# A linear-attention layer and a mixture of experts on one core: mix products left in PSUM until the input is added, shared expert on the routed experts' buffers, first weights loaded apart, stores issued by SyncE, and a new order of the pipelined stage

## The chip, the core and the metric

The kernel runs on one core of a Trainium2 chip. Its engines are TensorE (PE in the rows; PEld is its weight load), VectorE (DVE), ScalarE (ACT), GpSimd (POOL) and SyncE (SP), which here only issues transfers. Each engine runs its own instructions in program order and waits on semaphores for the others. Time is device time in microseconds (us); less is better. All data is fp32.

## What is computed

The input is 32 sequences of 256 tokens with 128 channels. Cut to what matters:

```
delta = shift(h) - h                          # the token before, minus this one
x1    = tanh(tanh((h + delta*mu) @ xl_w1.T) @ xl_w2.T + b)       # 5 groups of 32
mus   = einsum(x1, x_out_w) + x_bias          # five mixes r, w, k, v, g
r, k, v, g = (h + delta*mus_i) @ {r,k,v,g}_w.T
w     = tanh((h + delta*w_mu) @ w_w1.T) @ w_w2.T + w_b;  wd = exp(-exp(w))
scan over t:  o = r.S + sum(r*bonus*k)*v;   S = S*wd + k v
attn  = (groupnorm(o) * gn_w + gn_b) * silu(g) @ o_w.T
x     = layernorm(h + attn)
out   = layernorm(x + shared_ffn(x) + sum over the top 2 of 16 experts of weight * ffn_e(x))
```

Each expert is 128 to 512 to 128 channels with a ReLU.

## The kernel before

**Three stages.** In the first (to about 543 us) the tokens go through attention, router and shared expert in 16 units of two sequences (512 tokens); each token's row is scattered to DRAM at the place of its expert. In the second (to 856 us) 80 tiles of 256 rows go through their experts. In the third the two results of each token are read back, added and normalized, 16 units again.

**The first stage is a software pipeline.** A unit's work is cut into steps (a_: mixing and projections; b_: the scan, as five levels of products that double their length; c_: group norm, layer norm, router, slots, scatter; f_: shared expert). Each engine has a `body` that lists its steps with an offset. `pipeline(body)` runs the body once per i, and `at(d, step)` calls the step for unit i + d. I call one run of the body in the steady state a frame: one step of each kind, for several units. So the order of the work is written out by hand in the bodies; nothing reorders it later. `done(eng, name, u)` waits until unit u has raised that semaphore; `before(eng, name, u)` waits for the unit before it (or further back).

**The steps that matter here.** `a_adapt0` (PE, from the input tile hT), `a_adapt1`, then five products `mix` into the PSUM banks P0 and P1. VectorE's `a_mul` computes (product + bias) * delta and `a_add` adds the input; the sum `mixed` feeds the projections `a_r`, `a_decay_hid`, `a_k`, `a_v`, `a_g`. GpSimd's `b_step` 0 to 4 build the scan's levels, each waited for by PE's `b_level`, and each but the first waits for the level before. `c_attn` (PE) gives the attention output, and `c_z` (VectorE) adds the residual h_res. SyncE's loop issues for each u: the load of hT for unit u, a piece of expert weights, the load of h_res for unit u-1, which waits for `z` of unit u-2, and a padding row write; then it comes to hT of unit u+1. So the load of hT for unit X+3 stands behind `z` of unit X in SyncE's queue.

**Buffers.** The shared expert's hidden layer `hid` and the zero-filled v_flat and norm_work lie in the tile that later holds the experts' first weights (w_sb in the rows), so those weights are loaded in four pieces, each when its part is free. In the rows `w_ring` holds R, the scan's receptance.

Of the kernel before, what the change touches and what calls it, by code (L numbers as in the profile page):

```python
# [55 lines left out]
EARLY_COLS = MAT_AT["o_w"]  # L56


def build(nc, hidden, hidden_t, mats_dram, cols_dram, masks_dram, w1_dram, w2_dram, b2_dram, out):
# [8 lines left out]
    with ctx:  # L68
# [92 lines left out]
        hid = w1_flat[:, 2 * VD + 4 * UT:2 * VD + (4 + HC) * UT].rearrange("p (c t) -> p c t", t=UT)  # L161
# [18 lines left out]
        row_in = [rows[i // 4][i // 2 % 2][:, i % 2 * SUB:(i % 2 + 1) * SUB, :] for i in range(RING)]  # L180
        xTe = [x1T[0][:, i * ST:(i + 1) * ST] for i in range(2)]
        hide = two("hide", [128, HC, ST])
# [32 lines left out]
        def pipeline(body):  # L215
            for i in range(-2, UNITS + 3):
# [11 lines left out]
        def _(sp):  # L228
            sp.dma_start(mats[:, 0:EARLY_COLS], mats_dram[:, 0:EARLY_COLS]).then_inc(sem("weights"), 16)
            sp.dma_start(cols[:, :], cols_dram).then_inc(sem("weights"), 16)  # L230
# [10 lines left out]
            sp.wait_ge(sem("hT_edge"), 1)  # L241
            load_h(0)
# [3 lines left out]
            load_h(1)  # L246
            sp.wait_ge(sem("pad_rows"), 1)
# [4 lines left out]
            sp.dma_start(b2_sb[:, :, :], b2_dram).then_inc(sem("b2_in"), 16)  # L252
# [12 lines left out]
            at = lambda n: n // (HIDDEN + HC)  # L265
            done(sp, "o_ps", UNITS - 2)
# [13 lines left out]
            def load_rows(j, i):  # L280
                if not (isinstance(j, int) and j < RING):
                    sp.wait_ge(sem(f"e_back{i // 2}"), (j - i) * (2 * SUB * 16 // RING))
                for t in range(2):
                    sp.nop(nofuse=True)
                    r = sp.value_load(tile_ri[0:1, bass.ds(j + t, 1)], min_val=0, max_val=EXPERTS * CAP)
                    sp.dma_start(row_in[i + t], rows_dram[bass.ds(r, ST), :].rearrange("(s p) c -> p s c", p=128)).then_inc(sem(f"e_rows_in{i // 2}"), 16)
            for j in range(0, RING, 2):
                load_rows(j, j)
# [10 lines left out]


        @block.tensor
        def _(pe):
            mm = nc.tensor.matmul
            pe.wait_ge(sem("weights"), 32)
# [19 lines left out]
            def a_adapt0(u):  # L324
                if u == 0:
                    pe.wait_ge(sem("xl_parts"), 2)
                before(pe, "gate", u)
# [19 lines left out]
            def a_mix_w_r(u):  # L347
                done(pe, "adapt1a", u)
# [32 lines left out]
            def a_mix_g(u):  # L381
                done(pe, f"mul{MIX_V}", u)
# [152 lines left out]

            def body(at):
                at(1, a_mix_w_r)
                at(-1, c_attn)
                at(-2, f_up, 3)
                at(1, a_decay_hid)  # L540
                at(0, b_level, 3)
                at(1, a_w)
                at(1, a_r)
                at(-2, f_down, 0)
                at(0, b_level, 4)
                at(1, a_mix_k_v)
                at(-2, f_down, 1)
                at(1, a_mix_g)
                at(0, b_k_tok)
                at(-1, c_turn)  # L550
                at(1, a_k)
                at(0, b_kv)
                at(-1, c_logits)
                at(0, b_o_near)
                at(1, a_g)
                at(0, b_o_far)
                at(1, a_v)
                at(-1, f_up, 0)
                at(2, a_adapt0)
                at(1, b_level, 1)  # L560
                at(1, b_level, 0)
                at(-1, f_up, 1)
                at(2, a_adapt1)
                at(-1, c_place)
                at(-1, f_up, 2)
                at(1, b_level, 2)
# [66 lines left out]
        def _(act):  # L633
            A = nc.scalar.activation
            act.wait_ge(sem("weights"), 32)
# [158 lines left out]
            def body(at):  # L794
                at(-1, a_w)
                at(-1, a_r)
                at(-3, c_x1)
                at(-2, b_k_tok)
                at(-3, c_x1T)
                at(-1, a_k)  # L800
                at(-2, b_chunk_decay)
                at(-1, a_k_near)
                at(-1, a_decay)
                at(-1, a_r_near)
                at(-1, a_g)
                at(-3, c_logits)
                at(-2, b_o)
                at(-2, c_sq)
                at(-1, a_v)
                at(-3, f_hid, 0)  # L810
                at(0, a_adapt0)
                at(-3, f_hid, 1)
                at(-3, c_rows1)
                at(0, a_adapt1a)
                at(0, a_adapt1b)
                at(-2, c_aff)
                at(-3, c_top_exp)
                at(-3, f_hid, 2)
                at(-3, f_hid, 3)
                at(0, a_decay_hid)  # L820
# [41 lines left out]
            def f_store(u):  # L862
                done(act, "f_out", u)
                act.dma_start(out_v[:, u * TILES:(u + 1) * TILES, :], f_out[u % F_RING]).then_inc(sem(f"stored{u % F_RING}"), 16)  # L864
            for u in range(UNITS):
                f_norm(u)
                f_store(u)
            for i in range(F_RING):
                act.wait_ge(sem(f"stored{i}"), UNITS // F_RING * 16)
# [3 lines left out]
        def _(pool):  # L873
# [16 lines left out]
            pool.wait_ge(sem("weights"), 32)  # L890
# [514 lines left out]
```

## Time and profile before

| | us |
|---|---|
| median of 3 runs (lowest, highest) | 910.92 (910.13, 914.22) |
| the profiled execution's own time | 908.88 |
| its span, first to last instruction | 906.8 |
| mean granted TensorE clock | 0.946 of full |
| busy: PE, DVE, ACT, POOL | 785.1, 512.3, 491.9, 564.6 |

Busy shares are means over three stages of different kind. A PE that is busy is not always at its peak; the time in which it has nothing is what counts. "idle before" in a row is the engine's idle time ahead of the instruction, and the name behind the arrow is what ended it. SPq and ACTq are the queues by which SyncE and ScalarE issue transfers.

### The profile page before, as it was taken

The numbers are of one execution on the slowest core, as the hardware profiler recorded it, in microseconds if no ns is written. First come the engines' busy times: TensorE is split into PE (matmuls) and PEld (weight loads), VectorE is DVE, ScalarE is ACT, GpSimd is POOL, SyncE is SP. The second block draws the span as 40 slices with busy tenths as digits, with TensorE's granted clock in tenths as the row PEclk, the third lists the DMA queues.
The fourth block names the chain that finished last, engine by engine and source line by source line (L and its number), as shares of the span: only waits on it lengthen the run. The fifth ranks groups of instructions, "written<-read, shape, count | busy, mean of one in ns | idle before, by whom it ended". The sixth has DMA issues, their size and how long they took to land. (4 is left out here: it accounts for less than half of the span.)

```text
span 906.8 us, 24200 instructions
## 1 busy us (share of the span) xinstructions
PE 785.1 (87%) x8068; PEld 568.7 (63%) x8069; DVE 512.3 (56%) x1496; ACT 491.9 (54%) x1153; POOL 564.6 (62%) x709
## 2 busy tenths in 40 slices
PE   4687989988998899888987858999999999999493
PEld 1243545644565555554655537999999999999441
DVE  2436887889788978788775432333333333333076
ACT  1344667556655566555654314666555666566346
POOL 3334788788778787888788471555555554555444
PEclk9967999999999999999998678999999999999887
DMA  4001102211122112210213323222222222221294
GB/s 161 24 2 42 42 26 60 66 55 34 46 67 57 35 48 61 64 51 26 61 43 98 113 67 94 71 70 65 73 69 71 62 65 66 67 68 47 66 357 135
DMA packets 70244, 63.43 MB, mean 70 GB/s; under 512 B 8051, under 2 KB 61561, under 8 KB 70033
## 3 DMA queue, kind: packets, MB, share of 16 engines
q1 hardware_dynamic: 52496, 41.06, 15.9%
q0 software_dynamic: 9216, 17.07, 5.7%
q10 hardware_dynamic: 8448, 4.20, 1.6%
q8 instruction: 52, 0.85, 0.4%
q14 instruction: 32, 0.25, 0.1%
HBM read 38.75 MB, written 25.63 MB: 71 GB/s over the span
## 5 line engine op out<-in xcount | busy, mean ns | idle before, releaser
L974 POOL DMA_INDIRECT expert_results<-yw_all,rows x160 | 155.5, 972 | 155.3 <-ACT yw_all L837 130.6
L829 ACT ACTIVATE hide<-psB,w_ring 128x256 f32<-128x256 f32 x320 | 125.6, 475 | 67.9 <-PE psB L588 67.9
L599 PEld LDWEIGHTS psO<-w_sb,hide 128*128 128x128 f32 x1280 | 155.3, 192 | 4.6 <-issue 0.6
L599 PE MATMUL psO<-w_sb,hide 128*128 x1280 | 156.0, 275 | 0.1
L943 POOL DMA_INDIRECT dispatched_rows<-rows,slot x128 | 130.2, 1017 | 38.0 <-issue 31.0
L588 PE MATMUL psB<-x1T,w_ring 128*128 128x256 f32 x640 | 152.8, 382 | 0.2 <-DVE x1T L1264 0.2
L1277 DVE TENSOR_TENSOR K<-psO,b_sb 128x256 f32<-128x256 f32 x80 | 34.0, 425 | 175.1 <-PE psO L599 175.1
L588 PEld LDWEIGHTS psB<-x1T,w_ring 128*128 128x128 f32 x640 | 116.3, 192 | 13.3 <-issue 0.6
L921 POOL TENSOR_TENSOR w_ring<-w_ring,tot 128x128 f32<-128x128 f32 (+2 forms) x160 | 122.7, 788 | 0.0
L1022 DVE SCALAR_TENSOR_TENSOR mixed<-psP,cols,delta 128x512 f32<-128x512 f32 x80 | 59.7, 747 | 73.3 <-PE psP L318 42.5
L837 ACT ACTIVATE yw_all<-K,rows 128x128 f32<-128x128 f32 x160 | 55.4, 393 | 67.5 <-DVE K L1277 67.5
L792 ACT ACTIVATE w_sb<-psO,cols 128x512 f32<-128x512 f32 x64 | 43.7, 682 | 79.3 <-PE psO L524 78.9
L524 PE MATMUL psO<-x1T,mats 128*128 128x512 f32 x128 | 73.3, 656 | 12.4 <-ACT w_sb L792 12.4
L531 PEld LDWEIGHTS psO<-mats,w_sb 128*128 128x128 f32 x512 | 64.7, 206 | 20.7 <-issue 15.2
L1027 DVE TENSOR_TENSOR mixed<-mixed,hT 128x512 f32<-128x512 f32 x80 | 73.6, 921 | 2.2
L531 PE MATMUL psO<-mats,w_sb 128*128 128x128 f32 x512 | 70.4, 295 | 2.0 <-ACT w_sb L792 2.0
L908 POOL TENSOR_TENSOR tot<-tot 128x128 f32<-128x128 f32 (+4 forms) x80 | 22.2, 278 | 74.7 <-ACT R_near L679 42.3
L928 POOL TENSOR_TENSOR o_rstd<-o_var,minus_half 128x16 f32<-128x16 f32 x16 | 46.9, 2930 | 26.8 <-DVE o_var L1070 26.8
L1271 DVE COPY w_ring<-w_sb 128x516 f32 x80 | 34.4, 429 | 34.0 <-issue 34.0
L309 PE MATMUL psP<-mixed,mats 128*64 128x256 f32 x192 | 35.4, 449 | 19.7 <-DVE mixed L1027 19.7
L426 PEld LDWEIGHTS psB<-w_ring,K 64*32 64x32 f32 x2048 | 20.0, 109 | 47.0 <-issue 45.3
L426 PE MATMUL psB<-w_ring,K 64*32 64x64 f32 x2048 | 30.4, 228 | 17.5 <-POOL w_ring L921 17.5
(173 smaller groups left out, 1320.1 us busy)
## 6 DMA issues: line engine op xcount, KB each, us to landing
rows<-dispatched_rows SPq DMA_DIRECT2D x80, 132.0 KB
w_sb<-expert_results SPq DMA_DIRECT2D x8, 1024.0 KB, 13.0
hT<-in_hidden_t SPq DMA_DIRECT2D x16, 256.0 KB, 4.2
h_res<-in_hidden SPq DMA_DIRECT2D x16, 256.0 KB, 2.9
out<-w_sb ACTq DMA_DIRECT2D x16, 256.0 KB, 2.3
w_sb<-in_w SPq DMA_DIRECT2D x14, 256.0 KB, 4.4
expert_results<-yw_all,rows POOLq DMA_INDIRECT x160, 2.3
dispatched_rows<-pad_rows SPq DMA_DIRECT2D x17, 132.0 KB, 3.5
```

Source lines behind the costliest of these rows:

```text
L426: last = mm(to, k, r, start=True, stop=True, tile_position=(64 * b, 32 * c4))
L524: mm(O1, mat("shared_w1")[:, c * 128:(c + 1) * 128], x1T[u % 2][:, :], start=True, stop=True).then_inc(sem(f"hid_ps{c}"))
L531: last = mm(O1[:, j * 128:(j + 1) * 128], hid[:, c, j * 128:(j + 1) * 128], mat("shared_w2")[:, c * 128:(c + 1) * 128], start=(c == 0), st ...
L588: last = mm(up_ps(p)[:, c // 2, (c % 2) * ST:(c % 2 + 1) * ST], w1b[i % W_RING][:, c * 128:(c + 1) * 128], xTe[p], start=True, stop=True)
L599: last = mm(psO[:, p, s * 128:(s + 1) * 128], hide[p][:, c, s * 128:(s + 1) * 128], w2_sb[:, bass.ds(e, 1), c, :].rearrange("p e c -> p (e ...
L829: last = A(hide[p][:, c, :], psB[:, 2 * p + c // 2, (c % 2) * ST:(c % 2 + 1) * ST], ACT.Relu, bias=w1b[i % W_RING][:, HIDDEN + c:HIDDEN + ...
L837: last = A(yw[i][:, s, :], ye[p][:, s, :], ACT.Copy, scale=row_in[i][:, s, AT_W:AT_W + 1])
L921: last = G.tensor_tensor(r, r, l, ALU.mult)
L943: G.indirect_dma_start(rows_dram[:, :], bass.IndirectOffsetOnAxis(slot[u % 2][:, j, k:k + 1], 0), rows[k][u % 2][:, j, :], None).then_inc( ...
L974: G.indirect_dma_start(back_dram[:, :], bass.IndirectOffsetOnAxis(row_in[i][:, s, AT_DEST:AT_DEST + 1].bitcast(u32), 0), yw[i][:, s, :], N ...
L1022: V.scalar_tensor_tensor(mixed[MIX_BUF[n]][:, :, :], unflat((P0, P1)[MIX_BANK[n]]), col(f"x_bias{n}"), delta[:, :, :], ALU.add, ALU.mult). ...
L1027: V.tensor_tensor(mixed[MIX_BUF[n]][:, :, :], mixed[MIX_BUF[n]][:, :, :], hT[u % 2][:, :, 1:T + 1], ALU.add).then_inc(sem(f"mixed{n}"))
```

## The change

Parts, in the order of the diff below:

- hid lies in the routed experts' `hide` buffers, so the last piece of expert weights (experts 12 to 15) is loaded without waiting for the shared expert; the ring of row buffers is listed in another order, and only its last pair waits for the last `base_out`.
- The first weights (224 of 1160 columns) have a transfer and a semaphore of their own, and the first hT is loaded by ScalarE's queue. VectorE makes xl_prev and xl_cur first.
- `a_mul` writes its result back into the PSUM bank in place, and `a_add` takes it from there; the waits for the `mixed` buffers move from `a_mul` to `a_add`. `a_mix_g` waits for the sum of v instead of its product.
- b2 is added at the start of GpSimd's program and not after its pipeline.
- The stores of the last stage are issued by SyncE, behind its eight loads of expert results, and not by ScalarE.
- All four bodies are written in another order with other offsets.

```diff
-EARLY_COLS = MAT_AT["o_w"]
+FIRST_COLS, EARLY_COLS = MAT_AT["x_out_a"], MAT_AT["o_w"]
...
-        hid = w1_flat[:, 2 * VD + 4 * UT:2 * VD + (4 + HC) * UT].rearrange("p (c t) -> p c t", t=UT)
+        hide_both = sb("hide", [128, 2, HC, ST])
+        hide = [hide_both[:, i, :, :] for i in range(2)]
+        hid = hide_both[:, :, :, :].rearrange("p i c t -> p (i c t)").rearrange("p (c t) -> p c t", t=UT)
...
# sync
-            sp.dma_start(mats[:, 0:EARLY_COLS], mats_dram[:, 0:EARLY_COLS]).then_inc(sem("weights"), 16)
-            sp.dma_start(cols[:, :], cols_dram).then_inc(sem("weights"), 16)
+            sp.dma_start(mats[:, 0:FIRST_COLS], mats_dram[:, 0:FIRST_COLS]).then_inc(sem("first_weights"), 16)
+            sp.dma_start(cols[:, :], cols_dram).then_inc(sem("first_weights"), 16)
+            sp.dma_start(mats[:, FIRST_COLS:EARLY_COLS], mats_dram[:, FIRST_COLS:EARLY_COLS]).then_inc(sem("weights"), 16)
...
+            load_w1(-(-(2 * VD + 4 * UT) // (HIDDEN + HC)), EXPERTS)
...
-            load_w1(at(2 * VD), at(2 * VD + 4 * UT))
-            done(sp, "base_out", UNITS - 1)
-            load_w1(at(2 * VD + 4 * UT), EXPERTS)
+            load_w1(at(2 * VD), -(-(2 * VD + 4 * UT) // (HIDDEN + HC)))
...
+            def f_store(u):
+                done(sp, "f_out", u)
+                sp.dma_start(out_v[:, u * TILES:(u + 1) * TILES, :], f_out[u % F_RING]).then_inc(sem(f"stored{u % F_RING}"), 16)
+            for u in range(UNITS):
+                f_store(u)
...
# tensor: the body (ScalarE's, GpSimd's and VectorE's change in the same way)
-                at(1, a_mix_w_r)
-                at(-1, c_attn)
...
-                at(1, a_v)
-                at(-1, f_up, 0)
-                at(2, a_adapt0)
...
+                at(2, a_k)
+                at(0, c_attn)
+                at(1, b_o_far)
+                at(2, a_g)
+                at(2, a_v)
+                at(2, b_level, 1)
+                at(2, b_level, 0)
+                at(3, a_adapt0)
...
# scalar
+            act.dma_start(hT[0][:, :, 1:T + 1], hidden_t[:, 0:UB, :]).then_inc(sem("h_in0"), 16)
...
# gpsimd: moved from behind pipeline(body) to its front
+            pool.wait_ge(sem("b2_in"), 16)
+            pool.wait_ge(sem("late_weights"), 16)
+            G.tensor_tensor(b2_sb[:, :, :], b2_sb[:, :, :], mat("shared_b2").unsqueeze(1).broadcast_to([128, EXPERTS, C]),
+                            ALU.add).then_inc(sem("b2_ready"))
...
# vector
-                V.scalar_tensor_tensor(mixed[MIX_BUF[n]][:, :, :], unflat((P0, P1)[MIX_BANK[n]]),
-                                       col(f"x_bias{n}"), delta[:, :, :], ALU.add, ALU.mult).then_inc(sem(f"mul{n}"))
+                ps = unflat(psP[MIX_BANK[n]])
+                V.scalar_tensor_tensor(ps, ps, col(f"x_bias{n}"), delta[:, :, :], ALU.add, ALU.mult).then_inc(sem(f"mul{n}"))
...
-                V.tensor_tensor(mixed[MIX_BUF[n]][:, :, :], mixed[MIX_BUF[n]][:, :, :], hT[u % 2][:, :, 1:T + 1], ALU.add).then_inc(sem(f"mixed{n}"))
+                V.tensor_tensor(mixed[MIX_BUF[n]][:, :, :], unflat(psP[MIX_BANK[n]]), hT[u % 2][:, :, 1:T + 1], ALU.add).then_inc(sem(f"mixed{n}"))
```

In a steady frame TensorE comes from `c_attn` of unit X to `a_adapt0` of unit X+3, the pair that SyncE's loop links. Before, `c_attn` (L480) starts the following piece and `a_adapt0` (L332) stands 21 rows behind it:

```order
174 L480 MATMUL psO<-mats,w_sb 128x128 x4
175 L524 MATMUL psO<-x1T,mats 128x512
176 L309 MATMUL psP<-mixed,mats 64x256 x2
177 L426 MATMUL psB<-w_ring,K 32x64 x16
178 L367 MATMUL psP<-decay_hid,mats 64x256 x2
179 L309 MATMUL psP<-mixed,mats 64x256 x2
180 L531 MATMUL psO<-mats,w_sb 128x128 x8
```

The products of the mix, of the scan and of the shared expert follow `c_attn` there. The next piece, also of TensorE before, is the place of `a_adapt0`:

```order
192 L468 MATMUL psB<-state,w_ring 128x32 x14
193 L390 MATMUL psP<-v_wc,mixed 128x128 x4
194 L524 MATMUL psO<-x1T,mats 128x512
195 L332 MATMUL psP<-hT,xl_cur 64x256 x2
196 L332 MATMUL psP<-hT,xl_prev 64x256 x2
197 L426 MATMUL psB<-w_ring,K 32x64 x16
198 L426 MATMUL psB<-R_near,K_near 32x128 x16
199 L524 MATMUL psO<-x1T,mats 128x512
```

It comes ahead of `b_level` 1 and 0 (L426) there.

In the changed kernel the same two steps are `c_attn` (L493) and `a_adapt0` (L343); between them stand `b_o_far` (L481), `a_g` (L409), `a_v` (L403) and two levels (L439):

```order
209 L319 MATMUL psP<-mixed,mats 64x256 x2
210 L493 MATMUL psO<-mats,w_sb 128x128 x4
211 L481 MATMUL psB<-state,w_ring 128x32 x14
212 L409 MATMUL psP<-mixed,mats 128x512
213 L403 MATMUL psP<-v_wc,mixed 128x128 x4
214 L439 MATMUL psB<-w_ring,K 32x64 x16
215 L439 MATMUL psB<-R_near,K_near 32x128 x16
216 L343 MATMUL psP<-hT,xl_cur 64x256 x2
217 L343 MATMUL psP<-hT,xl_prev 64x256 x2
218 L537 MATMUL psO<-x1T,mats 128x512
```

`a_adapt0` has moved from far behind `c_attn` to close behind it, and `b_level` 1 and 0 of the same unit now stand ahead of it.

On VectorE, before, product and sum of the decay mix (L1022, L1027) and of r follow each other, and the sum has two inputs in SBUF:

```order
222 L1022 SCALAR_TENSOR_TENSOR mixed<-psP,cols,delta 128x512
223 L1027 TENSOR_TENSOR mixed<-mixed,hT 128x512
224 L1022 SCALAR_TENSOR_TENSOR mixed<-psP,cols,delta 128x512
225 L1027 TENSOR_TENSOR mixed<-mixed,hT 128x512
226 L1096 TENSOR_TENSOR z<-psO,h_res 128x512
```

In the changed kernel the two products (L1023) come first, r's ahead of the decay's, and both sums (L1034) read PSUM:

```order
242 L1219 TENSOR_SCALAR dest<-dest 128x8
243 L1023 SCALAR_TENSOR_TENSOR psP<-psP,cols,delta 128x512 x2
244 L1034 TENSOR_TENSOR mixed<-psP,hT 128x512 x2
245 L1227 TENSOR_TENSOR base_out<-psO,rows_1 128x512
246 L1059 COPY_PREDICATED pair<-masks,psB 128x32x8
```

The sum of the decay mix is now the fourth of these instructions and no longer the second.

At the end of SyncE's program, before, stand the loads of the results alone (L298):

```order
149 L298 DMA w_sb<-expert_results 128x8x256 x8
150 L68 UNCONDITIONAL_BRANCH
```

Nothing follows them. In the changed kernel the stores do (L304):

```order
148 L291 REGISTER_ALU
149 L291 COMPARE_AND_BRANCH
150 L300 DMA w_sb<-expert_results 128x8x256 x8
151 L304 DMA out<-w_sb 128x4x128 x16
152 L68 UNCONDITIONAL_BRANCH
```

All 16 stores stand behind the eighth load.

## Rows read from the trace of the kernel before

**Rows 1.** Windows, a frame: stretch, us; PE, PEld, DVE, ACT, POOL busy; PEclk, DMA, GB/s

```profile
262.80:292.20 29.40, 26.14 (x372) 15.97 (x371) 24.46 (x67) 17.62 (x38) 23.71 (x32) 1.00 0.18 52
```

**Rows 2.** Lines L1027, L1022 and L1096: ns min/median/max, first and last start

```profile
L1027 DVE TENSOR_TENSOR mixed<-mixed,hT x80: 665/692/2250, 18.2 to 472.7; 128x512 f32<-128x512 f32 x80
...
L1022 DVE SCALAR_TENSOR_TENSOR mixed<-psP,cols,delta x80: 736/750/754, 17.4 to 470.1; 128x512 f32<-128x512 f32 x80
...
L1096 DVE TENSOR_TENSOR z<-psO,h_res x16: 681/682/692, 77.8 to 512.2; 128x512 f32<-128x512 f32 x16
```

**Rows 3.** Timeline, PE, a steady frame: start us, us, engine, line, operation

```profile
265.82 1.12 PE L396 MATMUL psP<-mixed,mats 128*128 128x512 f32 x2
...
269.56 1.02 PE L524 MATMUL psO<-x1T,mats 128*128 128x512 f32 x2
...
271.52 0.46 PE L426 MATMUL psB<-w_ring,K 64*32 64x64 f32 x32
271.85 0.73 PE L426 MATMUL psB<-R_near,K_near 64*32 64x128 f32 x32
...
279.44 1.16 PE L480 MATMUL psO<-mats,w_sb 128*128 128x128 f32 x8
280.44 1.02 PE L524 MATMUL psO<-x1T,mats 128*128 128x512 f32 x2
282.81 0.65 PE L309 MATMUL psP<-mixed,mats 128*64 128x256 f32 x4 [1.35 <-DVE mixed L1027]
```

**Rows 4.** Timeline, VectorE and SyncE's queue, the same frame

```profile
283.97 0.68 DVE L1096 TENSOR_TENSOR z<-psO,h_res 128x512 f32<-128x512 f32 x1
...
285.97 0.37 SPq L235 DMA_DIRECT2D hT<-in_hidden_t  x1
```

**Rows 5.** Transfers of hT: one issue of that frame; then all 16, us to landing

```profile
hT<-in_hidden_t SPq DMA_DIRECT2D x1, 256.0 KB, 4.5
...
DMA to landing us min/median/max: 2.6/4.2/6.8
```

**Rows 6.** Timeline, ScalarE: table load for unit 0, first tanh of units 2 and 15

```profile
9.70 1.28 ACT L642 ACT_TABLE_LOAD   x1 [9.70 <-PE psP L332]
...
67.28 0.38 ACT L642 ACTIVATE adapt<-psP 128x256 f32<-128x256 f32 x1
...
449.77 0.38 ACT L642 ACTIVATE adapt<-psP 128x256 f32<-128x256 f32 x1
```

**Rows 7.** Timeline, GpSimd, the end of its first stage

```profile
489.94 1.21 POOL L921 TENSOR_TENSOR w_ring<-w_ring,tot 128x256 f32<-128x256 f32 x2
...
538.10 0.96 POOL L943 DMA_INDIRECT dispatched_rows<-rows,slot  x1 [0.30 <-issue]
```

**Rows 8.** Timeline, GpSimd, the last memset of the start

```profile
5.33 1.83 POOL L889 MEMSET w_sb<- 128x2048 f32 x1
```

**Rows 9.** Timeline, between the first and the second stage

```profile
541.04 0.37 SPq L264 DMA_DIRECT2D w_sb<-in_w  x1
...
548.12 1.08 PE L579 MATMUL psP<-mats,rows 128*128 128x128 f32 x4 [7.94 <-DMA rows<-dispatched_rows]
```

**Rows 10.** Timeline, SyncE's queue, ScalarE and VectorE in the last stage

```profile
855.62 18.45 SPq L298 DMA_DIRECT2D w_sb<-expert_results  x8
...
878.36 1.65 ACT L858 ACTIVATE w_sb<-w_sb,f_shift,f_rstd 128x128 f32<-128x128 f32 x4 [0.54 <-DMA out<-w_sb]
...
879.76 0.69 DVE L1305 TENSOR_TENSOR w_sb<-psO,base_out 128x512 f32<-128x512 f32 x1
...
881.84 0.69 DVE L1305 TENSOR_TENSOR w_sb<-psP,base_out 128x512 f32<-128x512 f32 x1
```

**Rows 11.** Windows of the last stage

```profile
862.00:864.00 2.00, 2.00 (x4) 0.77 (x3) 0.00 (x0) 0.00 (x0) 0.00 (x0) 0.50 1.10 353
```

**Rows 12.** DMA issues, the last stage's loads and stores: KB each, median us to landing

```profile
w_sb<-expert_results SPq DMA_DIRECT2D x8, 1024.0 KB, 13.0
...
out<-w_sb ACTq DMA_DIRECT2D x16, 256.0 KB, 2.3
```

More of the change, by code:

```diff
@@ L179, in build @@
         tile_ri = sb("tile_ri", [1, ETILES], i32)
-        row_in = [rows[i // 4][i // 2 % 2][:, i % 2 * SUB:(i % 2 + 1) * SUB, :] for i in range(RING)]
+        row_in = [r[:, i * SUB:(i + 1) * SUB, :] for r in (rows[0][0], rows[1][0], rows[1][1], rows[0][1]) for i in range(2)]
         xTe = [x1T[0][:, i * ST:(i + 1) * ST] for i in range(2)]
-        hide = two("hide", [128, HC, ST])
         ye = [K[i].rearrange("p (s c) -> p s c", c=C) for i in range(2)]
@@ L536, in body @@
             def body(at):
-                at(1, a_mix_w_r)
-                at(-1, c_attn)
[L539 to L556, printed above, removed]
-                at(1, a_v)
-                at(-1, f_up, 0)
-                at(2, a_adapt0)
[L560 to L566, printed above, removed]
+                at(2, a_k)
[6 more added lines that the diff above has]
+                at(3, a_adapt0)
+                at(-1, f_up, 3)
+                at(2, b_level, 2)
+                at(3, a_adapt1)
+                at(-1, f_down, 0)
+                at(3, a_mix_w_r)
+                at(2, b_level, 3)
+                at(-1, f_down, 1)
+                at(0, c_turn)
+                at(3, a_r)
+                at(3, a_decay_hid)
+                at(0, c_logits)
+                at(2, b_level, 4)
+                at(0, f_up, 0)
+                at(3, a_w)
+                at(2, b_o_near)
+                at(3, a_mix_k_v)
+                at(2, b_k_tok)
+                at(0, f_up, 1)
+                at(0, c_place)
+                at(2, b_kv)
+                at(3, a_mix_g)
+                at(0, f_up, 2)
             pipeline(body)
@@ L794, in body @@
             def body(at):
[L795 to L820, printed above, removed]
+                at(1, a_w)
+                at(-2, c_rows1)
+                at(-2, f_hid, 0)
+                at(-1, c_aff)
+                at(0, b_k_tok)
+                at(-2, f_hid, 1)
+                at(-2, c_top_exp)
+                at(0, b_chunk_decay)
+                at(1, a_r_near)
+                at(1, a_k)
+                at(1, a_decay)
+                at(1, a_k_near)
+                at(-2, f_hid, 2)
+                at(0, b_o)
+                at(0, c_sq)
+                at(1, a_g)
+                at(1, a_v)
+                at(2, a_adapt0)
+                at(-2, f_hid, 3)
+                at(2, a_adapt1b)
+                at(2, a_adapt1a)
+                at(-1, c_x1)
+                at(-1, c_x1T)
+                at(2, a_decay_hid)
+                at(-1, c_logits)
+                at(2, a_r)
             pipeline(body)
```

124 lines of the change are left out of this document (60 added, 64 removed).

## The prediction

> **What bounds the kernel now.** I took the chain of waits first. It is a chain in the first stage and the experts' matmuls in the second, where TensorE never pauses. No part of the change alters an instruction of the second stage, so I left it at its time. Then I took the windows of one frame of the first stage. A frame lasts 29.40 us, TensorE is busy for 26.14 of them, GpSimd for 23.71, VectorE for 24.46 [rows 1]. So TensorE idles 3.26 us per frame, and what a new order can win there is nearly that, 16 times. The timeline of the frame shows four such pauses; the longest is 1.35 us, when `a_decay_hid` waits for the sum of the decay mix (L1027) [rows 3].
>
> That sum is the VectorE instruction that varies: its minimum is 665 ns, its median 692, its longest 2250, while the sum of the same shape that takes one input from PSUM (L1096) stays between 681 and 692 in all 16 frames [rows 2]. The long ones fall on GpSimd's `b_step` instructions. The Trainium skill (SBUF — State Buffer, Who interferes with whom) has a rule for it: a VectorE instruction with two SBUF inputs contends with a GpSimd instruction that reads SBUF, and one with at most one SBUF input does not. By that rule every sum of the changed kernel costs about 0.69 us wherever the order puts it; were something else the cause, the long one could stay and bring its pause along, 13 times 1.35 us. L1096 speaks for the rule.
>
> **Part 1, mix products in PSUM.** Five products per frame keep their inputs; only the target changes. The nearest price is the same instruction with an SBUF target, 0.75 us (L1022, 736 to 754 ns [rows 2]). No row has VectorE writing to PSUM: below I bound it by 0.69 (an ordinary sum [rows 2]), above by 0.75 + 0.69 = 1.44, a second pass over the tile. I take 0.75, the row it is nearest to. One of the five sums per frame is a long one (2.25 at most) and comes down to 0.69, which takes 1.5 us per frame off VectorE and removes the cause of TensorE's 1.35 us pause. VectorE isn't the bound, so only the pause counts.
>
> **Part 2, the order.** I laid out one new frame with start-to-start distances of the old one. The chains I checked: mix products (1.13 us) to VectorE's two products and two sums, to `a_decay_hid`, to ScalarE's tanh, copy of r and exponential, to the next mixes; the second pair of mixes to `a_mix_g` and `a_k`; k to `b_step` 0. They fit between TensorE's 26.14 us of work with 0.2 to 0.7 us to spare. GpSimd needs 23.71 plus 0.30 ahead of each of eight scatters [rows 1, 7], 26.1 us; `b_step` 1 now directly follows 0, so it waits for `b_level` 1 in between, about 0.7 us. That makes 26.8 us: the frame's floor if nothing else waited.
>
> What is late next is a transfer. The load of hT for unit X+3 stands behind `z` of unit X in SyncE's queue, and `z` follows `c_attn` of X. Before, `a_adapt0` of X+3 came 20 us after `c_attn` of X, so the load was hidden. Now between their starts lies only this TensorE work: `c_attn` 1.00 (279.44 to 280.44), `b_o_far`, `a_g` and `a_v` 3.74 (three steps, 265.82 to 269.56), `b_level` 1 and 0 1.06 (271.52 to 272.58): 5.80 us [rows 3]. The load's chain is longer: `c_attn` 1.16 to its end [rows 3] and 0.13 to VectorE (a usual hand-over); start of `z` to the issue of hT 2.00 (283.97 to 285.97, with the issues of h_res and the padding ahead) [rows 4]; landing 4.5 in that frame [rows 5]; 0.13 to TensorE. Sum 7.92; in the frame before the second piece was 1.80, giving 7.72. TensorE therefore waits about 2.1 us ahead of `a_adapt0` in every frame: 26.14 - 5.80 + 7.8 = 28.2 us, with 7.8 between the two sums. Behind `a_adapt0` stand f_up 3, `b_level` 2, `a_adapt1` and all that follows; the wait covers the 0.7 us of `b_level` 2's own wait for GpSimd.
>
> The frames that this covers are those from the tanh of unit 2 to that of unit 15: 449.77 - 67.28 = 382.5 us for 13, 29.42 each [rows 6]. At 28.2 they take 366.6: **-15.9 us**. The first two frames are single chains through nearly empty engines; new steps ahead of `a_adapt0` (levels 1 and 0) stand against earlier r: 0, bounds -2 and +2.
>
> **Part 3, start.** The first tanh's table load begins at 9.70 [rows 6], after loads of 580 KB and v's mean. With 112 KB first, xl first and hT on another queue, what holds it next is the `zeroed` wait: the last memset ends at 5.33 + 1.83 = 7.16 [rows 8]. Bounds -2.5 and 0; I take **-2.0**, since nothing else in the trace comes between. b2's addition falls into the time in which GpSimd has no unit yet; uncovered it would cost its own length once, 4.5 us in the timeline.
>
> **Part 4, drain.** GpSimd ends its last `b_step` 3 at 491.15 and its last scatter at 539.06, 47.9 us later [rows 7]. The new order has one more unit's scatters behind that point: four units of eight at 1.26 = 40.3, `b_step` 4 1.6, o_rstd 2.9, two z_rstd 2.6, and about 3 of waiting for the last slots: 50.5 us, +2.6. Against that the way from the tanh of unit 15 to the end of `b_step` 3 shrinks, 41.4 before [rows 6, 7] and about 37 in my layout. Sum **-2.0**, bounds -7 and +4.
>
> **Part 5, to the experts.** The piece of w_sb at 541.04 goes ahead of the rows, and TensorE starts at 548.12, waiting for rows [rows 9]. That 1290 KB transfer (6.1 us to landing) now runs long before. **-1.5**, bounds -3 and 0. The shared expert on the hide buffers costs nothing: no one else uses them then.
>
> **Part 6, last stage.** ScalarE needs 1.65 us for a unit with 0.54 idle before it, 2.18 in all, VectorE starts a unit every 2.08 (879.76, 881.84) [rows 10]. Without ScalarE's issues VectorE sets the pace: 15 times 0.10, -1.5. But SyncE's eight loads of 1 MB end their issue only at 855.62 + 18.45 = 874.07 [rows 10], and they land a median of 13.0 us after issue, the stores on ScalarE's queue 2.3 [rows 12]. The 8.39 MB need, at the 353 GB/s of this stage [rows 11], until about 882. If stores land behind them, unit 4's normalization waits (878.36 before) until about 882.5, and VectorE's unit 8, which needs its buffer, starts at 884.2 and not 881.84 [rows 10]. Less VectorE's faster pace and the ACT lag of 1.7 us, the end moves **+0.5**, bounds -1.5 and +2.5. The Trainium skill (DMA: Bandwidth & Descriptors, Queues, rings and completion order) speaks against this edit: one issuing engine's ring is consumed in order, while an engine takes turns between the rings of two issuers. The 13.0 against 2.3 agrees; without that rule the term would be -1.5.
>
> **Sum.** -15.9 + 0 - 2.0 - 2.0 - 1.5 + 0.5 = -20.9 us against the profiled execution's 908.88 (span 906.8): 888.0. The three runs shown lie 1.3 to 5.3 above that execution, so I say **889 us** for a median.
>
> **Rivals.**
> A: the load isn't waited for. The shortest hT landing is 2.6 [rows 5], 1.9 less, which leaves 0.2; the frame falls to GpSimd's 26.8: another 13 x 1.4 = 18 us, 871. For it: the median of 4.2 includes frames of varied traffic. Against it: 4.5 in the steady frame with the same three neighbours.
> B, slower than before: the same wait, longer. The longest landing is 6.8 [rows 5]; the frame becomes 28.2 + 2.3 = 30.5, +30 us, 919. The point from which it decides is a landing of 6.1 us, where 13 frames of 29.8 eat the other terms. Against it: 6.8 falls in the crowded start.
> C: the slack of the mixes is used up. If a product into PSUM costs 1.44, the four instructions ahead of `a_decay_hid` grow by 1.4 and the second pair likewise, against 0.2 and 0.7 of slack: +1.9, 30.1 per frame, 914. A milder form, 0.8 us of small waits that I have not seen in a frame of some 100 steps, gives 29.0 and 899.
> D: VectorE or GpSimd contend elsewhere as before and the order wins nothing: 13 frames of 29.4, 905.
>
> **How the numbers follow.** Forecast (frame 27.7 to 28.7, 883 to 896): 0.53. A: 0.18. C mild: 0.16. D: 0.05. B and C full: 0.08. Faster by over 0.5% means below 906.4, slower above 915.5; half a percent is about what a measurement of this kernel tells from no change. Faster: 0.53 + 0.18 + 0.16 + 0.02 of D = 0.89; same 0.05; slower 0.06. The range reaches down to A and up to the milder C: 871 to 902; the forecast's own range is 883 to 896.
>
> **What would show it.** First tanh near 9 us. Starts of `a_adapt0`'s tanh 28.2 us apart, TensorE idle about 2 us ahead of it, with the DMA of hT as releaser, and none ahead of `a_decay_hid`. All 80 sums near 0.69, products near 0.75. The last scatter ending near 519, experts unchanged at 3.73 us per tile, ScalarE's fifth unit of the last stage some 4 us late behind a store. Wrong it would be if the frame shows another releaser in TensorE's longest pause, or if the products take over 1 us.

## The result, and the profile after

Over 11 runs of each, the changed kernel takes a median of 902.86 us (896.35 to 910.28) and the kernel before 910.92 (907.75 to 916.80): a ratio of 0.990, 95% interval 0.986 to 0.993. It is faster, but by 8 us and not by the 22 predicted; the median lies just above the range's end of 902. The profiled execution took 897.26 us (span 895.2, mean granted clock 0.942) against 888.0 in the prediction's sum. In a second comparison the ratio was 0.997 (0.993 to 1.000): 910.63 us, 12 runs from 903.56 to 917.09.

The wait that the prediction named is there. In TensorE's waits (us in total, times, longest) it stands first. The matmuls that wait for a sum of the mixes, `a_decay_hid` among them, waited 19.7 us in 14 times before and now 7.1 in 6, all before 99 us:

```profile
PE psP L343 <- DMA hT<-in_hidden_t: 25.5, 13, 2.3
```

The sums and products of the mixes, by line (busy us, mean ns of one), answer to [rows 2]. No sum is over 692 ns, where the longest was 2250, and a product into PSUM costs what one into SBUF did:

```profile
L1023 DVE SCALAR_TENSOR_TENSOR psP<-psP,cols,delta 128x512 f32<-128x512 f32 x80 | 58.5, 749 | 55.9 <-PE psP L328 55.9
L1034 DVE TENSOR_TENSOR mixed<-psP,hT 128x512 f32<-128x512 f32 x80 | 53.5, 685 | 6.9 <-PE psP L319 3.8
```

One frame is now the time from one `a_adapt0` on TensorE to the next. These windows of six frames answer to [rows 1]; the number behind POOL's is the granted clock:

```profile
89.95:120.04 30.09, 25.63 (x337) 13.79 (x337) 19.35 (x57) 16.80 (x37) 15.36 (x24) 0.83 0.11 32
120.04:147.95 27.91, 26.04 (x371) 16.26 (x371) 21.66 (x67) 17.48 (x38) 23.18 (x32) 1.00 0.19 54
147.95:176.21 28.26, 26.03 (x370) 16.26 (x371) 21.68 (x67) 17.48 (x38) 23.57 (x33) 1.00 0.19 54
176.21:206.16 29.95, 27.68 (x371) 16.79 (x371) 21.43 (x67) 17.37 (x38) 23.22 (x32) 0.94 0.18 51
235.72:263.58 27.86, 26.03 (x370) 16.25 (x371) 21.52 (x67) 17.58 (x38) 23.05 (x32) 1.00 0.19 55
263.58:294.96 31.38, 29.14 (x370) 17.98 (x371) 21.53 (x67) 17.49 (x38) 23.96 (x33) 0.89 0.17 49
```

I call the 11 frames from 120.04 to 437.53 settled: the pipeline is full, all have the same instructions, and each starts behind a pause of 1.56 to 2.27 us. Five of them are shown. Six of the 11 have the clock at 1.00 and last 27.85 to 28.26 us, 27.98 on the mean, as predicted (28.2). The other five last 29.11 to 31.38, because TensorE's own busy time grows from 26.03 to 27.6 or 29.1 at a clock of 0.94 or 0.89. I call them fallen and the six clean. Where inside the frame that happens, two-microsecond windows of the last one shown tell:

```profile
265.00:267.00 2.00, 2.00 (x36) 0.61 (x36) 0.29 (x2) 0.76 (x2) 0.73 (x1) 0.51 0.03 8
267.00:269.00 2.00, 2.00 (x9) 0.54 (x9) 1.76 (x8) 0.10 (x1) 1.90 (x6) 0.50 0.00 0
269.00:271.00 2.00, 2.00 (x11) 2.00 (x10) 0.82 (x5) 1.83 (x4) 2.00 (x2) 0.50 0.02 4
271.00:273.00 2.00, 2.00 (x13) 1.49 (x11) 0.00 (x0) 0.96 (x3) 1.24 (x1) 0.79 0.00 0
273.00:275.00 2.00, 2.00 (x47) 1.54 (x44) 1.38 (x3) 0.00 (x0) 0.95 (x3) 1.00 0.00 0
```

From 265.00 on, 1.4 us behind the end of the pause, the clock stands at 0.50, which is 1.2 of 2.4 GHz, and in the window from 273.00 it is back at 1.00. In the frames at 0.94 that stretch is about half as long. The timeline shows, for two other frames, the pause and the same two f_up matmuls (L537) with the clock fallen and with it full:

```profile
294.96 0.65 PE L343 MATMUL psP<-hT,xl_cur 128*64 128x256 f32 x4 [2.23 <-DMA hT<-in_hidden_t]
296.14 2.08 PE L537 MATMUL psO<-x1T,mats 128*128 128x512 f32 x2
...
235.72 0.65 PE L343 MATMUL psP<-hT,xl_cur 128*64 128x256 f32 x4 [2.01 <-DMA hT<-in_hidden_t]
236.74 1.12 PE L537 MATMUL psO<-x1T,mats 128*128 128x512 f32 x2
```

The start, the way to the experts and the last stage (ScalarE's table load, TensorE's first rows, then SyncE's queue, ScalarE's fourth and fifth unit, VectorE's ninth) answer to [rows 6, 9, 10]:

```profile
7.94 1.28 ACT L656 ACT_TABLE_LOAD   x1 [7.94 <-PE psP L343]
...
534.44 0.88 PE L592 MATMUL psP<-mats,rows 128*128 128x128 f32 x4 [5.14 <-DMA rows<-dispatched_rows]
...
841.70 18.52 SPq L300 DMA_DIRECT2D w_sb<-expert_results  x8
860.27 19.96 SPq L304 DMA_DIRECT2D out<-w_sb  x10
...
862.16 1.65 ACT L872 ACTIVATE w_sb<-hide,f_shift,f_rstd 128x128 f32<-128x128 f32 x4 [0.48 <-DVE f_shift L1332]
870.01 5.11 ACT L872 ACTIVATE w_sb<-hide,f_shift,f_rstd 128x128 f32<-128x128 f32 x13 [6.20 <-DMA out<-w_sb]
...
871.75 0.69 DVE L1312 TENSOR_TENSOR hide<-psP,base_out 128x512 f32<-128x512 f32 x1 [3.46 <-issue]
```

Against the kernel before's profiled execution, stretch by stretch:

| term | predicted | measured | from |
|---|---|---|---|
| 13 frames | -15.9 | -6.5 | 376.19 against 382.73, `a_adapt0` of unit 2 to that of 15 |
| first two frames | 0 | -1.5 | 55.54 against 56.99 |
| start | -2.0 | -1.8 | 5.80 against 7.57 |
| drain | -2.0 | -0.8 | last `a_adapt0` to end of last scatter, 90.98 against 91.77 |
| to the experts | -1.5 | -3.1 | 5.93 against 9.06 |
| experts | 0 | -0.2 | 307.26 against 307.50 |
| last stage | +0.5 | +2.3 | 53.5 against 51.2 |
| sum | -20.9 | -11.6 | 897.26 less 908.88 |

The 13 frames are the term that missed. The other six add up to -5.1 where I had -5.0, and that is luck: the way to the experts came out 1.6 us better, the first frames 1.5 better, the last stage 1.8 worse and the drain 1.2 worse.

### The profile page after: what moved, and what is told of

Its sections match the earlier page's. It is cut to its first block, busy times and chain, and to the rows that moved or that the text cites. A ratio compares the mean times of both kernels' runs of the same rounds, so it can differ in the third digit from the quotient of the medians.

```text
span 895.2 us, 24269 instructions
## 1 busy us (share of the span) xinstructions
PE 787.2 (88%) x8068; PEld 572.1 (64%) x8069; DVE 480.6 (54%) x1496; ACT 489.1 (55%) x1153; POOL 558.8 (62%) x709
## 4 chain that ended last, share of the span: by engine, by line
PE 73%; DMA 10%; DVE 5%; issue 4%; POOL 3%; ACT 2%; SPq 2%; DVEq 0%; POOLq 0%; ACTq 0%
PE psO L612 16%; PE psB L601 16%; PE psO L537 7%; DMA hT<-in_hidden_t 7%; PE psP L328 6%; PE psO L544 5%; PE psP L319 3%; PE psB L439 2%; PE psP L592 2%; PE psP L343 2%; PE psB L471 2%; PE psO L493 2%; PE psB L459 2%; POOL dispatched_rows L955 1%; PE psP L352 1%
## 5 line engine op out<-in xcount | busy, mean ns | idle before, releaser
L979 POOL DMA_INDIRECT expert_results<-yw_all,rows x160 | 157.3, 983 | 154.7 <-ACT yw_all L851 130.1
L933 POOL TENSOR_TENSOR w_ring<-w_ring,tot 128x128 f32<-128x128 f32 (+2 forms) x160 | 118.5, 761 | 0.0
L1023 DVE SCALAR_TENSOR_TENSOR psP<-psP,cols,delta 128x512 f32<-128x512 f32 x80 | 58.5, 749 | 55.9 <-PE psP L328 55.9
L537 PE MATMUL psO<-x1T,mats 128*128 128x512 f32 x128 | 78.4, 698 | 2.0 <-ACT hide L806 1.9
L544 PEld LDWEIGHTS psO<-mats,hide 128*128 128x128 f32 x512 | 62.8, 201 | 12.6 <-ACT hide L806 6.0
L544 PE MATMUL psO<-mats,hide 128*128 128x128 f32 x512 | 68.4, 290 | 2.8 <-ACT hide L806 2.8
L806 ACT ACTIVATE hide<-psO,cols 128x512 f32<-128x512 f32 x64 | 43.7, 683 | 34.4 <-PE psO L537 34.2
L1034 DVE TENSOR_TENSOR mixed<-psP,hT 128x512 f32<-128x512 f32 x80 | 53.5, 685 | 6.9 <-PE psP L319 3.8
L328 PE MATMUL psP<-adapt1a,mats 32*128 32x512 f32 x128 | 41.0, 718 | 6.7 <-ACT adapt1a L662 6.0
L439 PEld LDWEIGHTS psB<-w_ring,K 64*32 64x32 f32 x2048 | 20.5, 113 | 40.9 <-issue 39.1
L1059 DVE COPY_PREDICATED pair<-masks,psB 128x256 f32<-128x256 uint32 x64 | 31.9, 498 | 24.9 <-PE psB L439 23.4
```

Source lines behind the costliest of these rows:

```text
L328: mm(ps, w, a, start=True, stop=True, **kw).then_inc(sem(f"mix_ps{n}"))
L537: mm(O1, mat("shared_w1")[:, c * 128:(c + 1) * 128], x1T[u % 2][:, :], start=True, stop=True).then_inc(sem(f"hid_ps{c}"))
L544: last = mm(O1[:, j * 128:(j + 1) * 128], hid[:, c, j * 128:(j + 1) * 128], mat("shared_w2")[:, c * 128:(c + 1) * 128], start=(c == 0), st ...
L933: last = G.tensor_tensor(r, r, l, ALU.mult)
L979: G.indirect_dma_start(back_dram[:, :], bass.IndirectOffsetOnAxis(row_in[i][:, s, AT_DEST:AT_DEST + 1].bitcast(u32), 0), yw[i][:, s, :], N ...
L1023: V.scalar_tensor_tensor(ps, ps, col(f"x_bias{n}"), delta[:, :, :], ALU.add, ALU.mult).then_inc(sem(f"mul{n}"))
```

## The experiments

The theory: the pause of some 2 us in every frame was priced rightly, but behind it TensorE's clock falls in about half of the frames, and that is the miss. The rivals: the frames are long for another reason and the clock falls with it; or it is the late transfer and not the pause. Ratios are to the kernel before, run beside on the same device, with their 95% intervals.

**The changed kernel again.**

> The changed kernel once more, as the measure for the three that run beside it: 0.990 of the kernel before, 897 to 908 us, a mean granted clock of 0.93 to 0.94. The theory (pause and clock): 13 pauses of 1.6 to 2.3 us ahead of a_adapt0, and in some 5 to 7 of the 13 frames a clock that falls behind the pause, so frames of 28 us and of 29.5 to 31.4 us side by side. Were the long frames chance of one execution, this profile would show 13 frames near 28.2.

Measured: 0.997 (0.993 to 1.000), 910.63 us. Of the 11 settled frames five lasted 27.8 to 28.3 at clock 1.00; six were longer, the longest by 6.2 us of TensorE's busy time:

```profile
205.85:240.18 34.33, 32.27 (x370) 20.03 (x371) 21.50 (x67) 17.47 (x38) 22.68 (x32) 0.80 0.15 44
```

The clean frame is a constant of the kernel; how many frames fall, and how far, differs from one execution to the next. The profile of the kernel with its stores by ScalarE (below), whose first stage is the same, has only two fallen frames of 11: its 13 frames take 370.28 us, where the first execution has 376.19 and this one 382.71.

That is a part of the spread of 14 us and not all of it. Of the 16.4 us between the profiled spans of this execution and the first, 6.5 lie in the 13 frames and 7.3 in the drain (98.26 against 90.98). The last of the pauses stands at the drain's start. Here the clock fell behind it, and TensorE's busy time in the drain is 5.2 us longer (77.84 against 72.64); in the first execution it stayed at 1.00 there.

```profile
448.28:452.28 4.00, 4.00 (x18) 2.85 (x17) 2.04 (x11) 2.47 (x6) 4.00 (x6) 0.50 0.00 0
```

**Load hT one unit earlier.**

```
-            for u in range(2, UNITS):
-                load_h(u)
+            load_h(2)
+            for u in range(2, UNITS):
+                if u + 1 < UNITS:
+                    load_h(u + 1)
                 ...
                 load_res(u - 1)
```

> SyncE issues the load of hT one unit earlier, ahead of the load of h_res, so it no longer stands behind the wait for z. Theory (the pause ahead of a_adapt0 and the clock that falls behind it cost 13 x 2.0 and some 9 us): no wait for the load, frames at 26.8 to 27.2 with the clock at 1.00, 13 frames 350 us where the changed kernel has 376: profiled 870 to 876 us, 0.960 to 0.968 of the kernel before. Rival (the load was late, but the frames are held by GpSimd's own chain or the order, the clock falls by itself): the wait goes to another instruction, frames 28 to 29, 890 to 898 us. Rival (only the 2 us go, the clock still falls in half of the frames): frames 27 to 28.5, some 880 us.

Measured: 0.961 (0.958 to 0.963), 876.25 us, all six runs within 3.3 us. The wait for hT is gone, all 11 settled frames last 27.07 to 27.23 at clock 1.00, and the 13 take 352.42:

```profile
222.25:249.32 27.07, 26.34 (x377) 16.12 (x370) 23.25 (x67) 17.63 (x39) 23.48 (x32) 1.00 0.20 58
```

Of the 23.8 us between these 13 frames and the changed kernel's 376.19, the pause itself explains 11 x 0.9 = 9.8, the five fallen frames 149.63 - 5 x 27.98 = 9.7, and the first two of the 13 (58.70 against 54.32) 4.4.

**The pause filled.** Five matmuls stand in front of the wait; the load comes as late as before.

```
                 before(pe, "gate", u)
+                pe.nop(nofuse=True)
+                if u >= 3:
+                    for _ in range(5):
+                        mm(P1[:, 0:256], mats[:, 0:128], mats[:, 0:256], start=True, stop=True)
                 h_in(u)
```

> The changed kernel, with five matmuls of 256 columns into P1 (their result is overwritten by a_adapt0) in front of the wait for hT from unit 3 on, some 1.4 us of work in the place of the pause of 2; the load comes as late as before. Theory (the pause lets the clock fall): clock 1.00 in all 13 frames, each at 27.9 to 28.3, 13 frames some 366 us where the changed kernel has 376; profiled 886 to 889 us, 0.978 to 0.982 of the kernel before, as the prediction had it. Rival (the clock falls for another reason, and the frames are long for it): the same 376 us and 897 us or more, with 0.94 as the mean clock.

Measured: 0.981 (0.979 to 0.984), 895.68 us where the changed kernel beside it took 910.63. The clock stayed at 1.00 in all 11 settled frames. They weren't shorter than the clean frames, because five matmuls cost 2.28 us and not 1.4, and in four frames hT was later still:

```profile
175.62:203.94 28.32, 28.32 (x381) 17.99 (x380) 21.50 (x68) 17.37 (x38) 23.43 (x32) 1.00 0.19 54
232.26:261.69 29.43, 28.40 (x382) 18.02 (x381) 21.38 (x68) 17.60 (x38) 24.29 (x34) 1.00 0.18 52
```

15 us came back from adding work to the engine that is the bound. Of the 15.6 between the two profiled spans 8.9 lie in the 13 frames and 5.7 in the drain.

**The pause filled in part**: two matmuls in place of five.

> The changed kernel with two matmuls in front of the wait for hT in the place of five: by their cost with five (TensorE's busy time 28.32 less 26.04 a frame, 0.46 each) some 0.9 us of work, so a pause of 1.0 to 1.4 us is left of the 2.0, and the load is as late as in the changed kernel. Theory (the length of the pause decides): clock 1.00 in all settled frames, each 27.9 to 28.3, 13 frames 366 to 368 us, 888 to 891 us, 0.974 to 0.978 of before: the predicted time. Rival (the late hT, not the pause, or any filling short of the whole pause fails): falls in about half of the frames as without filling, 0.99 of before.

Measured: 0.974 (0.972 to 0.977), 889.57 us, with pauses of 0.77 to 1.28 us left and the clock at 1.00 in all 11 settled frames; 13 frames take 368.0, where 366.6 was predicted. So with the load as late as in the changed kernel, the predicted frames come once the clock is kept. That the whole meets the predicted 889 is luck besides: the other terms miss by up to 3 us each and add up to -5.1 against -5.0.

```profile
PE psP L347 <- DMA hT<-in_hidden_t: 12.9, 13, 1.3
...
287.65:315.99 28.34, 27.10 (x375) 16.92 (x375) 21.38 (x68) 17.46 (x38) 23.49 (x33) 1.00 0.19 54
```

**A made pause with hT early.** A load of 16 bytes, issued when `b_level` 0 has ended, holds `a_adapt0` back (on top of the early load):

```
+                    done(sp, "level_ps0", u)
+                    sp.dma_start(scratch[:, :], cols_dram[0:1, 0:4]).then_inc(sem("first_weights"), 16)
...
                 h_in(u)
+                if u >= 3:
+                    pe.wait_ge(sem("first_weights"), u * 16)
```

> The early load of hT stays, but from unit 3 on a_adapt0 also waits for a load of 16 bytes that SyncE issues when b_level 0 has ended: hT is there in time, and TensorE pauses 2 to 3 us all the same at the place of the changed kernel's pause. Theory (any pause of this length lets the clock fall in part of the frames, whatever causes it): clean frames of 26.35 + pause = 28.5 to 29.3, and beside them frames 1.5, 3.1 or 6.2 us longer at a clock of 0.94, 0.89 or 0.80; sum of the 13 frames 380 to 390 us, spread of the times 10 us or more, some 0.995 of before. Rival (the clock falls with the late transfer, by what the load of hT does beside TensorE, not with the pause): all frames clean at 28.5 to 29.3, clock 1.00, spread of the times under 4 us.

Measured in the first run: 0.968 (0.963 to 0.973), but on a device on which every frame also had a stop of another kind (below), so it is no answer.

> The pause made by a load of 16 bytes ahead of a_adapt0, hT loaded early, once more; the first run had 13 pauses of 1.40 to 1.55 us at this place beside the stop of 2.5 us at the state, so that it does not tell the two apart. Theory (the clock falls behind a pause, whatever makes it): with this pause alone frames of 26.1 + 1.45 = 27.6, and some of them longer by 1.55 or 3.1 us at a clock of 0.94 or 0.89; since the pause is shorter than the changed kernel's 2.0 fewer may fall: 0 to 5 of 11. Rival (the late hT transfer is what matters): all at 27.6 with clock 1.00.

Measured in the second: 0.967 (0.965 to 0.969), 882.55 us. Pauses of 1.40 to 1.61 us and no fall in 11 frames:

```profile
PE psP L351 <- DMA scratch<-in_cols: 19.0, 13, 1.6
...
229.49:257.02 27.53, 26.03 (x370) 16.24 (x371) 22.02 (x69) 17.67 (x39) 23.32 (x32) 1.00 0.19 56
```

**The same pause, longer**: three such loads in place of one.

> As the kernel with the pause made by a load of 16 bytes (13 pauses of 1.40 to 1.61 us, clock 1.00 in all 11 settled frames, 882.6 us), but SyncE issues three such loads one behind the other and a_adapt0 waits for all three, so the pause grows by two issues of some 0.4 us to 2.2 to 2.4; hT itself is there long before. Theory (a pause of the changed kernel's length makes the clock fall in part of the frames whatever causes it): clean frames of 28.3 to 28.5, some 3 to 7 of 11 longer by 1.55 or 3.1 us at a clock of 0.94 or 0.89, spread of the times over 7 us, 0.98 to 0.99 of before. Rival (the clock falls only where hT comes late): all frames at 28.3 to 28.5 with clock 1.00, spread under 4 us, 13 frames some 370 us, 892 us and 0.977 of before.

Measured: 1.004 (1.001 to 1.006), 916.23 us, 910.64 to 925.41. The pauses are 1.99 to 2.10 us, hT is there long before, and seven of 11 settled frames fall. I had expected a longer pause (2.2 to 2.4) and a smaller loss (0.98 to 0.99). Three frames, clean, fallen and fallen furthest:

```profile
PE psP L352 <- DMA scratch<-in_cols: 26.6, 13, 2.1
...
239.65:267.73 28.08, 26.04 (x370) 16.26 (x371) 21.94 (x68) 17.57 (x38) 23.19 (x32) 1.00 0.20 53
325.43:356.60 31.17, 29.14 (x370) 18.02 (x371) 21.79 (x68) 17.49 (x38) 23.60 (x32) 0.89 0.18 49
356.60:390.92 34.32, 32.28 (x370) 20.04 (x371) 21.88 (x68) 17.47 (x38) 22.93 (x32) 0.80 0.15 44
```

So the late transfer is not the cause; the pause is, whatever makes it. Against the shorter made pause 7.6 us more of waiting (26.6 less 19.0) cost 34 us, each beside a kernel before of 912 to 913. Of the 32.3 between the two profiled spans 26.6 lie in the 13 frames and 6.7 in the drain, whose first quarter has a clock of 0.72 here and of 1.00 there.

**The mixes alone**: the kernel before, with the products in PSUM and a_add of V moved up behind its product.

> The kernel before with the products kept in PSUM and nothing else but a_add of V moved up behind its product. If the prediction's part on the mixes holds by itself: sums at 0.69, no pause ahead of a_decay_hid, 13 frames of 29.42 become 28.1 to 28.4, 0.981 to 0.986 of before. Rival (the 1.35 us turn up in another wait of the old order, since GpSimd's chain or ScalarE ends last there): frames 29.0 to 29.4, 0.995 to 1.0 of before.

Measured first, on the device with the extra stop: 1.009 (1.006 to 1.012).

> The kernel before with the products in PSUM, once more beside the same. The first run gave 1.009 of before with frames of 33.3 and 38.1 side by side, under the stop that the trace calls remote. If the old order has no place for the products in PSUM (a_add of V now holds P1 and VectorE's queue): frames over 29.42 without the stop too, ratio 1.005 to 1.015. If the loss came of the stop: frames 28.1 to 29.4 and 0.981 to 1.0.

Measured on a device without it: 0.981 (0.978 to 0.983), 894.26 us, and frames of 28.06 to 28.21:

```profile
237.71:265.77 28.06, 26.08 (x371) 15.95 (x370) 22.77 (x68) 17.50 (x39) 23.01 (x31) 1.00 0.19 54
```

The median of the 11 settled frames falls from 29.44 to 28.08, by 1.36 us, about the pause of 1.35 ahead of `a_decay_hid` [rows 3], and TensorE no longer waits there in them. This part alone, in the old order, beats the whole change (0.990 and 0.997).

**The old mixes in the new order**, with the early load: product to SBUF, sum in place.

> The changed order with the early load of hT (0.961 of before, frames of 27.08 with TensorE busy 26.35), and the mixes again as before: product written to SBUF, the sum in place there, so that VectorE's two-input sums read two SBUF tiles beside GpSimd. Theory (in this order TensorE has other work between the mixes and what reads them, so the sums' place is cover only): sums up to 2.3 us again, VectorE's busy time 1 to 2 us a frame higher, frames at 27.1 to 27.5, 0.961 to 0.967 of before. Rival (the products in PSUM are what shortens the frame): the 1.35 us ahead of a_decay_hid come back, frames at 28.4, 0.980 of before.

Measured first, with the extra stop: 0.961 (0.956 to 0.966).

> The changed order with early load and the mixes as before (product in SBUF, sum in place), once more: the first run had frames 0.55 us longer on the mean than the kernel with PSUM mixes beside it (13 frames 408.6 against 401.3 us), both under the stop. Theory (TensorE has other work between the mixes and their readers in this order, so their place is cover only): frames 27.1 to 27.6, ratio 0.961 to 0.967. Rival (the products in PSUM shorten the frame by the whole 1.35 us): frames 28.4, 0.980.

Measured without it: 0.971 (0.968 to 0.973), 885.83 us, frames of 27.54:

```profile
226.31:253.85 27.54, 26.41 (x375) 16.16 (x370) 23.82 (x67) 17.63 (x39) 23.92 (x32) 1.00 0.20 58
```

Sums reach 1985 ns again. Against 27.09 the frame loses 0.45 us, a third of the 1.36; the new order covers the rest. The frames are as my theory had them, the ratio isn't: of the 11.1 us between the two profiled spans 5.3 lie in the 13 frames, the rest in the first two frames (+1.9), the drain (+2.2) and the experts (+1.4), which I had left out. All three vary as much between two executions with the same first stage: the first frames 53.63 and 55.91, and in the changed kernel the drain 90.98 and 98.26, the experts 307.3 and 308.6. So these profiles can't tell whether the old mixes cost anything there.

**Stores by ScalarE again.**

```
             for u in range(UNITS):
                 f_norm(u)
+                f_store(u)
```

> The stores of the last stage go back to ScalarE's queue, nothing else. Theory (stores stand behind the eight loads in SyncE's ring and ScalarE's fifth unit waits for them): the last stage, from the first load of back to the end, falls from 53.5 to some 51.2 us, ScalarE's fifth unit comes 22.7 us behind the first load and not 28.3; the whole is 2 us shorter, 0.987 of the kernel before. Rival (the last 2.3 us were the loads' own time, set by the DMA engines' rate of about 350 GB/s): 53.5 us as now, no change of the whole.

Measured: 0.993 (0.990 to 0.996), 906.38 us, 892.64 to 916.41. The time can't tell 1.6 us under the falling clock, the trace can: the last stage takes 51.9 and not 53.5 (53.1 to 54.5 in all traces with the stores by SyncE from devices without the extra stop), and ScalarE's fifth unit comes 23.4 us behind the first load and not 28.3:

```profile
862.13 1.65 ACT L864 ACTIVATE w_sb<-hide,f_shift,f_rstd 128x128 f32<-128x128 f32 x4 [1.27 <-DMA out<-w_sb]
```

I had expected 51.2 and 22.7. This execution is the fastest of its 11: its pauses are 1.57 to 2.22 us, and only two settled frames fell, one of them this:

```profile
147.74:178.70 30.96, 29.14 (x370) 17.97 (x371) 21.57 (x67) 17.48 (x38) 23.55 (x32) 0.89 0.18 49
```

**Both mends together.**

> The early load of hT and the stores by ScalarE together. If the two act in different stages and add: frames 27.08 as with the early load alone, last stage 51.9 instead of 53.5; profiled 873 us, ratio 0.9590, and this is the shortest kernel of the study. If the store's place in SyncE's ring is hidden by something else now: the 0.9606 of the early load alone.

Measured first: 939.9 us and 0.952 (0.946 to 0.957), beside 990.8 for the kernel before. In a frame ScalarE and VectorE stand idle until something that the trace calls remote. Their waits show this stop 12 and 13 times, up to 5.2 us, and TensorE's clock is below 1.00 in all 11 settled frames:

```profile
ACT K L705 <- remote: 57.3, 12, 5.2
DVE state L1066 <- remote: 48.3, 13, 5.2
...
239.70:270.98 31.28, 28.10 (x379) 17.28 (x371) 23.06 (x67) 17.52 (x39) 23.49 (x33) 0.95 0.19 55
```

> The early load of hT and the stores by ScalarE once more. In the first run of this kernel ScalarE and VectorE stood idle once in every frame, until one instant for both (264.01 and 263.88 in the frame that began at 239.70), released by something that the trace calls remote, and TensorE behind them for 2.5 us; the kernel before ran 8.8% longer beside it than beside the run of the early load alone (990.8 and 912.1 us are its medians). If that stop belongs to the device: none here where the kernel before takes 912, frames 27.08, clock 1.00, ratio 0.959. If it belongs to this kernel: frames of 30 to 32 us again, and a ratio of 0.952.

Measured on another device: 0.959 (0.956 to 0.961), 875.08 us, frames of 27.07 to 27.21, last stage 51.86. None of the kernels run elsewhere shows a wait for remote, so the stop went with that device, or with the one session on it, and not with the kernel. This is the shortest kernel of the study, 37 us below the kernel before; from the early load alone (0.961) it can't be told by the time.

## Why the prediction was wrong

**What bounds the kernel** held: the first stage's frame is where the time moved, and the experts kept theirs.

**Part 1** held in each number: products 0.749, all sums under 0.70, pause gone. By itself it gives 1.36 us per frame.

**Part 2** is the step that failed, and only in one half. "TensorE therefore waits about 2.1 us ahead of `a_adapt0` in every frame" is what happened (1.56 to 2.27, 25.5 us in all, DMA of hT as releaser), and with the clock full the frame is 27.98. But "At 28.2 they take 366.6" assumed that TensorE's 26.14 us of work keep their length behind such a pause. They took 376.2: +8.6 for the five frames in which the clock fell, +2.3 for the two frames before the pipeline is full, -1.3 for the six clean ones. I had read the granted clock of a steady frame of before and carried it over to a kernel whose longest pause grew from 1.35 us to 2. The trace of before shows the effect once, in one of its 11 settled frames (31.03 us from `a_adapt0` to `a_adapt0` where the others take 29.4 to 29.7). Its pause ahead of `a_decay_hid` and a window behind it:

```profile
222.40 0.65 PE L309 MATMUL psP<-mixed,mats 128*64 128x256 f32 x4 [1.37 <-DVE mixed L1027]
...
226.00:228.00 2.00, 2.00 (x12) 2.00 (x11) 1.39 (x11) 1.30 (x4) 1.27 (x2) 0.54 0.87 190
```

I had not asked why that frame was longer. No rival named this. The nearest in time, the mild C of 899, had the wrong mechanism: no small waits came. The proof is that the 13 frames came to 368.0 us once two matmuls had cut the pause to 0.77 to 1.28 us, with the load still late.

The Trainium skill (TensorE: Matmul & The Clock Gate, HAM oscillation — how this bites in real kernels) tells of a kernel whose clock swings between the two levels because its TensorE waits for loads. The windows of 0.50 behind the pause agree. That kernel's waits are put at some 3 to 5 us, and here the clock fell behind 1.8 to 2.3. I hadn't weighed that section.

**Rival A** (the load isn't waited for, 871) fell as a forecast and was right as a price: without the wait the frame is 27.1 and the kernel takes 876. Its floor of 26.8 for GpSimd was 0.3 short. **B** and **D** didn't come. **First frames, drain, start**: inside their bounds in the profiled execution. The drain's 90.98 was a lucky one: with the same first stage it took 93.88 and 98.26 in two others, the last 6.5 us above the kernel before's and beyond the bound of +4. The clock that fell behind the last pause is part of it.

**Part 5**: -3.1 is just past the bound, not the middle. In all other traces with the new order of loads the way from the last scatter to TensorE's first rows takes 5.7 to 6.0 us. With the old loads it took 9.06 in the kernel before and 7.48 with PSUM mixes (10.31 on the device with the extra stop). So the loads are worth at least 1.5; what made the two old ones differ stays open.

**Part 6**: the mechanism was right (the stores land behind the loads, and the fifth unit waits for one, 5.6 us late where I said some 4), the size near the upper bound: +2.3. Undone, 1.6 of it returns.

## What to carry to other kernels

When a change leaves one pause in TensorE's work longer than any before it, price the pause twice: its own length, and the clock behind it. The granted clock of before is no measure for a kernel with another longest pause. Then look for what stands ahead of the late load in its queue, since here one load moved ahead of another's wait was worth 34 us on the device where the whole change brought 1.5. And run parts alone: this change held a part that by itself was worth more than the sum.

## What the runs showed of the hardware

A fall of the clock behind a pause costs TensorE 1.5, 3.1 or 6.2 us of busy time in the frame (26.04 becomes 27.6, 29.1 or 32.3). In four executions with one long pause a frame (1.56 to 2.27 us) 2, 5, 6 and 7 of 11 settled frames fell. All 20 fell behind pauses of 1.81 us or more, of which there were 37; behind the 7 shorter ones none did, nor behind the 26 pauses of 0.77 to 1.61 us in three other kernels. The kernel before, with 1.35 ahead of `a_decay_hid` and three shorter ones around it, had one of 11. Above 1.8 us the length alone doesn't decide which frame falls: in the first execution of the changed kernel 1.81, 1.83, 2.23, 2.23 and 2.27 us stood ahead of the fallen frames, 1.56 to 2.07 ahead of the clean ones, and in the second a frame behind 2.24 stayed clean. What decides it stays open.

Filling the changed kernel's pause with useless matmuls made it 1.6% faster (895.68 against 910.63 us on one device).

One device of the four on which experiments ran had a stop of ScalarE and VectorE in every frame, of a kind that the trace calls remote, and the five kernels run there were 7 to 12% longer than elsewhere. A comparison on it turned the verdict on the mixes round: 1.009 there and 0.981 elsewhere. What that stop is, no run here shows.
